# Decoding w1 and w2 with one ScalarE instruction per step for both blocks of a tile

## What is computed

```
w1, w2, w3 = NF4_TABLE[q] * scale                  # 16-entry table; w1, w2: 2752 x 1024, w3: 1024 x 2752
h = layernorm(x) * (1 + ca) + sa
x = x + ga * (h @ w_masked.T)
h = layernorm(x) * (1 + cb) + sb
h = silu(h @ w1.T) * (h @ w2.T)
x = x + gb * (h @ w3.T)
```

## Time and profile before

| what | value |
|---|---|
| median of 3 runs | 1578.53 us (1578.36 to 1578.96) |
| the profiled execution | 1579.52 us |
| its span, first to last instruction | 1577.4 us, mean granted clock 0.996 |
| PE busy | 1541.8 us, 98% of the span |
| DVE busy | 1034.4 us, 66% |
| ACT busy | 987.1 us, 63% |
| matmuls | 7200 |
| DMA queue 1 | 344.76 MB, 64.8% of 16 engines |

### The profile page before, as it was taken

How to read it: one execution, slowest core, us unless ns; L and a number is a source line. 1 busy time by engine, 2 the same in 40 slices (tenths; PEclk the granted TensorE clock), 3 DMA queues, 4 the chain that set the end, 5 groups by cost and what they waited for, 6 DMA issues and landing times.

```text
span 1577.4 us, 19154 instructions
## 1 busy us (share of the span) xinstructions
PE 1541.8 (98%) x7200; PEld 1271.3 (81%) x7200; DVE 1034.4 (66%) x1495; ACT 987.1 (63%) x1282; POOL 5.5 (0%) x10
## 2 busy tenths in 40 slices
PE   5889999999999999999999999999999999999998
PEld 3667888888888888888888888888888888888887
DVE  5777786555645455447666666666875758857677
ACT  3455675998898888884897988886333432333320
POOL 0000000000000000000000000000000000000000
PEclk9999999999999999999999999999999999999999
DMA  9985322565535555443777787786787968858866
GB/s 366 369 284 197 122 94 88 177 207 199 193 127 192 164 180 175 147 142 108 251 230 237 210 250 209 212 248 181 251 299 265 335 201 300 332 203 294 305 223 206
DMA packets 170139, 345.97 MB, mean 219 GB/s; under 512 B 14752, under 2 KB 65344, under 8 KB 170048
## 3 DMA queue, kind: packets, MB, share of 16 engines
q1 hardware_dynamic: 170048, 344.76, 64.8%
HBM read 249.77 MB, written 94.93 MB: 219 GB/s over the span
## 4 chain that ended last, share of the span: by engine, by line
PE 92%; DMA 3%; DVE 2%; ACT 1%; issue 1%; SPq 0%; ACTq 0%; DVEq 0%
PE ps L1898 10%; PE ps L1897 10%; PE ps L1896 10%; PE ps L1970 9%; PE ps L1969 9%; PE ps L1971 9%; PE ps L1907 9%; PE ps L1909 9%; PE ps L1908 9%; PE ps L1814 3%; PE ps L1815 3%; PE ps L1816 3%; DMA wmod<-wmod 2%; PE ps L1771 2%; PE ps L1754 1%; DMA x_d<-x 1%
## 5 line engine op out<-in xcount | busy, mean ns | idle before, releaser
L841 ACT ACTIVATE w_raw<-w_raw 128x1024 f32<-128x1024 f32 x287 | 304.6, 1061 | 9.1
L1896 PE MATMUL ps<-ffn_in_hi,w_hi 128*128 128x512 f32 x688 | 268.6, 390 | 0.0
L1898 PE MATMUL ps<-ffn_in_hi,w_lo 128*128 128x512 f32 x688 | 267.8, 389 | 0.0
L1897 PE MATMUL ps<-ffn_in_lo,w_hi 128*128 128x512 f32 x688 | 267.7, 389 | 0.0
L1969 PE MATMUL ps<-t_hi,s_hi 128*128 128x512 f32 x616 | 239.6, 389 | 0.0
L1970 PE MATMUL ps<-t_lo,s_hi 128*128 128x512 f32 x616 | 239.6, 389 | 0.0
L1971 PE MATMUL ps<-t_hi,s_lo 128*128 128x512 f32 x616 | 239.6, 389 | 0.0
L1907 PE MATMUL ps<-x_m_hi,stream_hi 128*128 128x512 f32 x604 | 235.0, 389 | 0.0
L1908 PE MATMUL ps<-x_m_lo,stream_hi 128*128 128x512 f32 x604 | 235.0, 389 | 0.0
L1909 PE MATMUL ps<-x_m_hi,stream_lo 128*128 128x512 f32 x604 | 235.0, 389 | 0.0
L1087 ACT ACTIVATE s_hi<-s_raw 128x1408 fp32r<-128x1408 f32 x56 | 77.4, 1383 | 231.4 <-DVE s_raw L1602 190.8
(11 more groups left out here) (140 smaller groups left out, 2083.8 us busy)
## 6 DMA issues: line engine op xcount, KB each, us to landing
s_raw<-h_d SPq DMA_DIRECT2D x96, 704.0 KB, 5.3
stream_raw<-t_d SPq DMA_DIRECT2D x150, 256.0 KB, 3.4
t_d<-combined SPq DMA_DIRECT2D x106, 256.0 KB, 2.6
wmod<-wmod SPq DMA_DIRECT2D x12, 2048.0 KB, 15.5
t_raw<-w_d SPq DMA_DIRECT2D x88, 256.0 KB, 6.3
w_codes<-w12q SPq DMA_DIRECT2D x41, 512.0 KB, 5.2
h_d<-h_tile SPq DMA_DIRECT2D x44, 256.0 KB, 2.4
h_d<-up_c SPq DMA_DIRECT2D x44, 256.0 KB, 3.2
```

Of the source, the lines that this page charges most:

```text
L841: act.activation(RAWF[r], RAWF[r] if j else RQ[r][:], ACT.Prelu, bias=bias, scale=sign, alpha=slope).then_inc(line_ready, 1)
L1896: pe.matmul(acc, RH[r][:, k, :], HH[:, b, k, :], start=(k == 0), stop=False)
L1897: pe.matmul(acc, RH[r][:, k, :], HL[:, b, k, :], start=False, stop=False)
L1898: last = pe.matmul(acc, RL[r][:, k, :], HH[:, b, k, :], start=False, stop=(k == C - 1))
```

## The change

ACT's chain is run over both blocks of a tile at once. The two blocks lie next to each other in memory (the ring is renamed as two pairs, same addresses), each step is one activation of 128 partitions x 2048 columns, and `lines(n)` first waits for the codes of both blocks. The first half of the steps (4) stands where block 0's eight steps stood, the second half where block 1's stood. Ahead of the last `input2` of the first kind, two steps over both blocks take the place of three steps over block 0. `finish` waits for the tile's eighth step, for either block. The tail tile keeps steps of 1024 columns.

```diff
-    raw_kb = (168, 172, 160, 164)
-    RQ = [at(f"w12_codes_{i}", [C * P], I32, kb) for i, kb in enumerate(raw_kb)]
-    RAW = [at(f"w12_raw_{i}", [C, P], F32, kb) for i, kb in enumerate(raw_kb)]
-    RAWF = [r[:].rearrange("p c h -> p (c h)") for r in RAW]
+    CODES = [at(f"w12_codes_{i}", [2, C * P], I32, kb) for i, kb in enumerate((168, 160))]
+    PAIR = [at(f"w12_raw_{i}", [2, C, P], F32, kb) for i, kb in enumerate((168, 160))]
+    RAW = [pair[:, w] for pair in PAIR for w in range(2)]
...
-                sp.dma_start(RQ[r][:], w12q[2 * n + w]).then_inc(codes_loaded[r], 16)
+                sp.dma_start(CODES[n % 2][:, w, :], w12q[2 * n + w]).then_inc(codes_loaded[r], 16)
...
-            def lines(n, w, first=0, last=NL):
+            def lines(n, first=0, last=NL):
 
-                r, J = ring(n, w), job(n, w)
-                act.wait_ge(codes_loaded[r], 16 * ((n + 1) // 2))
+                ws = 2 if n < FULL else 1
+                raw = PAIR[n % 2][:, 0:ws].rearrange("p w c h -> p w (c h)")
+                for w in range(ws):
+                    act.wait_ge(codes_loaded[ring(n, w)], 16 * ((n + 1) // 2))
                 for j in range(first, last):
                     sign, bias, slope = STEPS[j]
                     if j:
-                        act.wait_ge(line_ready, NL * J + j)
-                    act.activation(RAWF[r], RAWF[r] if j else RQ[r][:], ACT.Prelu,
+                        act.wait_ge(line_ready, NL * (n - 1) + j)
+                    act.activation(raw, raw if j else CODES[n % 2][:, 0:ws, :], ACT.Prelu,
                                    bias=bias, scale=sign, alpha=slope).then_inc(line_ready, 1)
...
-            lines(1, 0, 0, 3)
+            lines(1, 0, 2)
             input2(HALF_TILES - 1)
...
-                lines(n, 0, 3 if c == 0 else 0)
+                lines(n, 2 if c == 0 else 0, NL // 2)
                 silu(c, 0)
                 if 1 <= c <= HALF_TILES:
                     input2(HALF_TILES + c - 1)
-                lines(n, 1)
+                lines(n, NL // 2)
                 silu(c, 1)
-            lines(FULL, 0)
+            lines(FULL)
             silu(END, 0)
...
-                dve.wait_ge(line_ready, NL * (J + 1))
+                dve.wait_ge(line_ready, NL * n)
```

## The result

The changed kernel takes 1583.53 us (median of 6 runs, 1582.68 to 1585.50) against 1578.74 us (6 runs, 1578.25 to 1579.17): a ratio of 1.0031, 95% interval 1.0021 to 1.0042. It is slower by 4.8 us. The forecast was 1583.7 us.

A forecast was written before the change was run, and what follows sets the result against it. PE was taken to bound the kernel, so ACT's savings return nothing. A 3.8 us stall at chunk 1 plus 1.4 us for a clock fall made 5.2 us on 1578.53: 1583.7 us, range 1580.0 to 1586.0.

The forecast's parts named there:

- What bounds the kernel: Whole run: PE is busy 1541.8 of 1577.4 us, so nothing that ACT saves can come back as time.
- The step: ACT's chain: a merged 2048-column step takes 1.915 us, 1.945 from start to start, against 2.186 for two old steps.
- The stall: Start of chunk 1: PE waits for block 0 of tile 1, 3.75 us, or 3.8 with the longer first matmul.
- The later chunks: Chunks after chunk 0: tiles are ready with 3.5 us to spare, 4.5 from chunk 9 on; priced at nothing.
- T + 19.1: Later chunks with modulation: T is the chunk's start; DVE's part is ready 19.1 us after it, wanted at T + 22.68.
- the margin: Chunks with modulation: 3.5 us to spare between DVE's part being ready and the next chunk's start.
- the five sums in chunk 10: DVE in chunk 10: tile 0's sums wait for stores, about 6.2 us together, making the silu 1.1 us late.
- The clock: PE around the stall at chunk 1: the clock falls to half, 1.4 us lost, with ends 0 and 3.2.
- The first rival: Chunk 1's start: the stall without a fall of the clock, 1582.3 us (1581.9 to 1582.9); chance 0.27.
- No stall that counts: Second half of tile 1's chain: the 4.96 us lead is enough, time stays at 1578.5 us; chance 0.14.
- A second stall: Chunks 2 to 9 or `make_h`: half a microsecond missing in each of eight chunks, 4 us more, 1587.7 us; chance 0.11.
- The sum for chunk 1: ACT in chunk 1: first half runs from 289.9 to 297.6, done before the silu may start at 298.4.

The follow-up runs named there:

- experiment 2: The changed kernel with tiles 1 and 2 decoded block by block in 1024-column steps, merged from tile 3 on: 1578.85 us, ratio 0.9999 to the kernel before.
- experiment 1: The changed kernel with tile 1 decoded block by block in 1024-column steps, later tiles merged: 1579.70 us, ratio 1.0005 to the kernel before.
- experiment 3: Only tile 1 merged, tiles 2 to 21 decoded block by block as before the change: 1584.23 us, ratio 1.0035 to the kernel before.
- experiment 7: The kernel of experiment 6 with eight idle matmuls in PE's gap ahead of chunk 1: 1580.90 us, ratio 1.0014 to the kernel before.
- the second filled gap: Second run of the changed kernel with 16 idle matmuls where PE would wait for tile 1: 1583.10 us, ratio 1.0026 to the kernel before.
- Experiment 9: Tile 1 block by block; later tiles with two merged steps ahead of the first silu and six behind, or one and seven: 1588.68 and 1638.54 us.
- the filled gap: The changed kernel with 16 idle matmuls where PE would wait for tile 1, run twice: 1583.00 and 1583.10 us.
- experiment 6: The changed kernel with both silus of chunk 0 after tile 1's last merged step: 1582.63 us, ratio 1.0024 to the kernel before.
- the split 1 and 7: Tile 1 block by block; later tiles with one merged step ahead of the first silu and seven behind: 1638.54 us, ratio 1.0375 to the kernel before.

## Why the prediction was right

- **What bounds the kernel.** Right: 32.6 us less work on ACT brought nothing back, and no experiment got under the kernel before. The best version with merged steps (experiment 2) equals the kernel before.
- **The step.** Taken as 1.915 us, measured 1.918 (1.908 for the first), 1.945 from start to start. The Trainium skill ("ScalarE: Activation LUTs", "What ACT_TABLE_LOAD costs") would give an estimate of 1.892; the trace is 0.026 longer, as the rows of before had it. ACT's busy time fell by 32.6 us where 33 were forecast.
- **The stall.** The step that carried the forecast. Expected 3.75 us from start to start, measured 3.78. Its terms hold one by one with the 0.8 us by which the execution lies earlier: `input2` at 272.72 (273.5 forecast), the second half at 280.86 (281.65), DVE's low part at 291.87 (292.65). Experiments 1, 3 and 7 show that this stall sets the time: without it the loss is gone, tile 1 alone brings all of it, and with the clock kept a stall shorter by 1.8 us makes the time 2.2 us shorter (experiment 7 beside the second filled gap).
- **The later chunks.** No PE wait after 293 us. The part of a tile was forecast at T + 19.1. In the timeline of DVE:

```profile
333.55 1.22 DVE L1146 SCALAR_TENSOR_TENSOR w_raw<-w_raw,w_scale 128x1024 f32<-128x1024 f32 x1 [10.71 <-ACT w_raw L842]
...
335.60 1.23 DVE L1153 TENSOR_TENSOR w_lo<-w_raw,w_hi 128x1024 fp32r<-128x1024 f32 x1
```

  It ends at 336.83. T is 5.64 us ahead of that chunk's silu at 323.33, so 317.69, and the part is ready at T + 19.1. Experiment 9 ate up the margin: its waits came where the sum had them, 0.4 us larger from start to start, for the terms named there. One price of DVE was mis-sized without effect: the five sums in chunk 10 were to take 6.2 us and make the next silu 1.1 us late. They took 3.5 us (from 515.93 to 519.46), their wait for the store was 0.32 us in place of 2.95, and that silu came on time:

```profile
518.14 1.32 DVE L1167 TENSOR_TENSOR combined<-w_raw_first,w_raw_first 128x512 f32<-128x512 f32 x2 [0.32 <-DMA t_d<-combined]
```

- **The clock.** Forecast: a fall, 1.4 us lost, ends 0 and 3.2. In the three profiles of the change it fell each time, and lost 2.9, 1.7 and 1.5 us. Against the filled gap in the same set the median of the change is 1.6 us higher. The price was mis-sized for the profiled execution, about right for the median. That it fits so well is partly luck: it was the price of one other gap, and the same gap costs 1.5 to 2.9 us here. The first rival (the stall with no fall) is out as the usual case; one run of the first six, at 1582.68 us, lies where it would put the time.
- **The other rivals.** "No stall that counts" fell with the step's 1.918 us. Its bound was a slip: by the prediction's own terms (3.8 us, eight steps) the change falls below 3.2 us from a step of 1.84 us on, not 1.87. "A second stall" did not come in the changed kernel, but it was nearer than I thought: once the first stall is taken away, tile 2 is 0.7 us late (experiment 1). The sum for chunk 1 had used a start that the stall itself had put off.

What was missed was in the experiments' sums: a wait costs 0.25 us more than its idle time in the view of waits, the silu's wait for DVE's `h_tile`, and the clock's falls at short gaps.

## What to carry to other kernels

Merging two chains makes both ready at the end, so the first consumer loses the lead that the first block had. Compare that lead (4.96 us here) with how much later the first block will be ready (8.6 us here), and do it at the start of a stage, where no backlog covers it. An engine that is off the path gives nothing back when it gets faster. Where a gap on PE can't be avoided, count a possible fall of the clock on top of it, and remember that a stall can hide the next one.

## What the runs showed of the hardware

- A gap of 1.86 us was followed by a fall of the clock 1.1 us after PE was back at work (experiment 6), and with the gap filled the profile shows none (experiment 7). I had rows for 3.19 and 4.94 us only. But the gap's length alone doesn't decide. In the profile of the split 1 and 7, nine of the eleven gaps from 2.29 to 3.92 us went with a fall, in the gap or up to 1.4 us behind it, and two did not: those that end at 315.38 (3.06 us) and at 421.23 (2.29 us). Of these windows the first lies behind the one and the second holds the other; the third lies behind the gap of 2.35 us that ends at 340.69. What parts them stays open.

```profile
315.00:340.00 25.00, 22.96 (x104) 1.00 0.48 160
400.00:430.00 30.00, 27.71 (x131) 1.00 0.49 163
341.00:367.00 26.00, 24.26 (x104) 0.93 0.44 146
```

- The eight gaps of 1.28 to 1.59 us in that profile were followed by none, nor were the eleven of 0.32 to 1.56 us in the other profile of experiment 9. The longest of those lies in this window:

```profile
490.00:550.00 60.00, 58.44 (x258) 1.00 0.49 168
```

- The same gap costs different amounts in different executions, 1.5 to 2.9 us, and the fall comes now ahead of the first matmul behind it, now 1.2 us after. The runs spread accordingly: the change's first six over 2.8 us, those with the filled gap over 1.6. Part of the spread is older than the gap, since the same work starts up to 2.2 us apart in the profiles (the waits end at 291.41 and at 293.56).
- Small activations that don't wait for each other start 0.95 us apart at 1024 columns, dependent ones 1.093. By the Trainium skill ("ScalarE: Activation LUTs", "What ACT_TABLE_LOAD costs"), activations back to back overlap by about 93 ns. By that, the trace agrees (1.05 - 0.95 = 0.10 us) for independent ones, and the dependent chain shows none of it. Two chains in turn cost 1.90 us per pair of steps, a merged step 1.945, two dependent steps 2.186: the order alone saves on ACT all that merging saves.
